# Four chained blocks on one core: norms 1 to 3 in flat steps, low parts one step behind, and the mask and code loads in another order

## What is computed

```
x = x + A0(layernorm(x))     # product with a float32 weight, masked in 32x32 blocks
x = x + F0(layernorm(x))     # product with an int4 weight times a scale, plus a bias
x = x + A1(layernorm(x))     # NF4 weights (16 levels, one scale per 64) with LoRA: q+k+v,
                             # output projection, gate/up with silu, down
x = x + F1(layernorm(x))     # gate/up/down after fake quantisation to fp4 blocks of 16
```

## Time and profile before

| | |
|---|---|
| median of 3 runs | 831.2 us |
| the profiled execution | 829.33 us |
| its span | 828.0 us |
| TensorE (PE) busy | 726.4 us, 88% |
| VectorE (DVE) busy | 569.7 us, 69% |
| ScalarE (ACT) busy | 443.8 us, 54% |
| GpSimd (POOL) busy | 191.2 us, 23% |
| mean TensorE clock granted | 0.955 of full |

### The profile page before, as it was taken

The page is one execution under the profiler, slowest core; times in us unless marked ns, Lnnn a source line. Parts: engine busy times, 40 slices in busy tenths (PEclk is TensorE's granted clock), DMA queues, the critical chain, the costliest instruction groups (busy, mean ns, idle before and its releaser), DMA issues.

```text
span 828.0 us, 11306 instructions
## 1 busy us (share of the span) xinstructions
PE 726.4 (88%) x4136; PEld 538.7 (65%) x4136; DVE 569.7 (69%) x1083; ACT 443.8 (54%) x575; POOL 191.2 (23%) x176
## 2 busy tenths in 40 slices
PE   1898875989999998889998998798999799959998
PEld 1565532656767766657665776575777588947886
DVE  4779976653697788889897985568553434477773
ACT  4778787555876867787666611354322111224542
POOL 0214000021263452535544444122001100000000
PEclk9999966999999999999998999999999899988999
DMA  7736688765466676757655102012001220200001
GB/s 279 223 118 210 198 267 281 249 223 179 133 214 214 203 227 205 238 172 268 216 176 162 65 38 73 26 40 61 16 1 38 61 61 25 65 10 13 25 26 39
DMA packets 56039, 110.55 MB, mean 134 GB/s; under 512 B 9888, under 2 KB 20800, under 8 KB 55984
## 3 DMA queue, kind: packets, MB, share of 16 engines
q1 hardware_dynamic: 42560, 78.43, 29.4%
q10 hardware_dynamic: 9040, 17.30, 6.3%
q0 software_dynamic: 4384, 14.09, 5.9%
HBM read 91.65 MB, written 18.15 MB: 133 GB/s over the span
## 4 chain that ended last, share of the span: by engine, by line
PE 54%; DVE 21%; issue 9%; ACT 8%; DMA 6%; SPq 1%; ACTq 1%; POOL 0%; DVEq 0%; POOLq 0%
PE bank L1122 13%; PE bank L1123 13%; PE bank L1124 13%; PE bank L1229 3%; ACT hot L1528 2%; DVE hot L1774 2%; DVE x L1897 2%; DMA wide_buf<-in_down_flat 2%; DVE bank L1800 2%; PE bank L1417 2%; ACT c L1487 2%; DVE q_a L1847 1%; PE bank L1271 1%; PE bank L1242 1%; DVE q_r L1841 1%
## 5 line engine op out<-in xcount | busy, mean ns | idle before, releaser
L1528 ACT ACTIVATE hot<-rep,levels 128x2048 f16<-128x2048 f16 x96 | 193.6, 2057 | 16.9 <-ACT c L1487 11.0
L1122 PE MATMUL bank<-zt_h,w_h 128*128 128x512 f32 (+1 forms) x232 | 93.3, 402 | 2.5 <-DVE zt_l L1885 2.0
L1124 PE MATMUL bank<-zt_h,w_l 128*128 128x512 f32 (+1 forms) x232 | 91.4, 394 | 0.0
L1123 PE MATMUL bank<-zt_l,w_h 128*128 128x512 f32 (+1 forms) x232 | 91.2, 393 | 0.0
L1229 PE MATMUL bank<-hot,diag 128*32 128x512 f16 x1160 | 79.7, 406 | 2.2 <-ACT hot L1528 2.2
L1122 PE MATMUL bank<-w_h,xq_h 128*128 128x512 f32 (+1 forms) x192 | 74.3, 387 | 5.9 <-DVE w_l L1916 3.6
L1123 PE MATMUL bank<-w_l,xq_h 128*128 128x512 f32 (+1 forms) x192 | 72.0, 375 | 0.0
L1124 PE MATMUL bank<-w_h,xq_l 128*128 128x512 f32 (+1 forms) x192 | 71.9, 375 | 0.0
L2041 POOL TENSOR_TENSOR q_a<-q_a,q_m 128x384 f32<-128x384 f32 (+3 forms) x34 | 35.7, 1051 | 107.6 <-DVE q_m L1668 107.6
L1229 PEld LDWEIGHTS bank<-hot,diag 128*32 128x32 f16 x1160 | 26.4, 100 | 46.3 <-issue 25.7
L2097 POOL TENSOR_TENSOR at_l<-ztok,at_h 128x512 fp32r<-128x512 f32 x28 | 37.4, 1337 | 80.6 <-ACT at_h L1560 80.5
(11 more groups left out here) (222 smaller groups left out, 1688.4 us busy)
## 6 DMA issues: line engine op xcount, KB each, us to landing
rep<-codes SPq DMA_DIRECT2D x58, 512.0 KB, 4.6
codes<-c SPq DMA_DIRECT2D x29, 256.0 KB
raw<-in_codes_gu_t ACTq DMA_DIRECT2D x14, 512.0 KB, 5.7
sc<-in_scales_gu_t SPq DMA_DIRECT2D x56, 128.0 KB, 4.1
raw<-in_codes_attn_t ACTq DMA_DIRECT2D x8, 512.0 KB, 4.4
raw<-in_codes_down_t ACTq DMA_DIRECT2D x7, 512.0 KB, 6.5
sc<-in_scales_down_t SPq DMA_DIRECT2D x28, 128.0 KB, 3.0
wide_buf<-in_gate_flat SPq DMA_DIRECT2D x5, 512.0 KB, 4.2
```

Source lines behind the costliest of these rows:

```text
L1122: PE.matmul(psum, lh, rh, start=first, stop=False, **kw)
L1123: PE.matmul(psum, lh, rl, start=False, stop=False, **kw)
L1124: return PE.matmul(psum, ll, rh, start=False, stop=last, **kw)
L1528: S.activation(hots[plan.slot[hot_ring(t), (t, m)]][:], codes_in_place(t), ACT.Relu, bias=bias, scale=slope).then_inc(sem("ramp_act"), 1)
```

## The change

1. `stages` is written in flat steps: 24 tiles (ln, n) in one sequence and 26 steps. Step s holds the low part of tile s-2, the norm of tile s, the product of tile s-3, the turn of tile s, tsplit of tile s-1, and the add of tile s-4.
2. `PE_LOWS` goes from 3 to 2: norm 3 (ln 2) takes its low parts on VectorE (`tdiff`).
3. The mask: `mask_sum` ahead of `known 0 0`; the weight comes in four loads, and `mask_mul k` waits for its own; the parts of chunks 0 and 1 are made as before by ScalarE and POOL (`MASK_LOWS` = 2), those of chunks 2 and 3 by a copy and a subtraction on VectorE; the first product waits for each chunk where it needs it.
4. Codes and x: `ship 0` is issued on ACT's queue, and x tiles 4 to 7 are loaded on SP's queue behind `spread 0`.
5. Both sides start one step later (`late=1`).
6. `until` leaves its loop before the side step once the weights are there, so the last low parts come ahead of the maximum that stood between.

```diff
-PE_LOWS = 3
+PE_LOWS = 2
+MASK_LOWS = 2
 class Side:
-    def __init__(self, gen, rate=1.0):
-        self.gen, self.rate, self.owed = gen, rate, 0.0
+    def __init__(self, gen, rate=1.0, late=0.0):
+        self.gen, self.rate, self.owed = gen, rate, -late * rate
 ...
         spread(0)
+        p.add("load_rest")
         spread(1)
 ...
             next(nf4)
+            if made[0] > i:
+                break
             for side in sides:
                 side.step()
 ...
+    def turn_step(ln, n):
+        p.add("turn", ln, n)
+        turn_bank(("ln", ln, n), split_done(ln, n))
+    def low_step(ln, n):
+        p.add("tlow" if ln < PE_LOWS else "tdiff", ln, n)
 ...
     def stages():
-        turned = multiplied = added = None
-        for ln, blk in ((0, 1), (1, 2), (2, None)):
-            for n in norm_turn(ln):
-                if ln == n == 0:
-                    for k in range(KD):
-                        p.add("mask_mul", k)
-                if added and added[1] % HN == HN - 1:
-                    known(added[0], added[1] // HN)
-                if turned and turned[0]:
-                    product(*turned)
-                if multiplied and multiplied[0]:
-                    add(*multiplied)
 ...
+        tiles = [(ln, n) for ln in range(3) for n in range(NT)]
+        def behind(step, by):
+            return tiles[step - by] if 0 <= step - by < len(tiles) else None
+        for step in range(len(tiles) + 2):
+            now, high, low, ready, multiplied = (behind(step, by) for by in range(5))
+            if low:
+                low_step(*low)
+            if now:
+                norm(*now)
+            if step == 0:
+                for k in range(KD):
+                    p.add("mask_mul", k)
+                for k in range(KD):
+                    p.add("mask_low" if k < MASK_LOWS else "mask_rest", k)
+            if ready and ready[0] < 2:
+                product(ready[0] + 1, ready[1])
+            if now:
+                turn_step(*now)
+            if high:
+                p.add("tsplit", *high)
+            if multiplied and multiplied[0] < 2:
+                add(multiplied[0] + 1, multiplied[1])
+            if step < HN // 2:
+                stats(0, HN + 2 * step)
+                stats(0, HN + 2 * step + 1)
+            yield
 ...
+    p.add("mask_sum")
     known(0, 0)
-    p.add("mask_sum")
-    weave(stages(), Side(itertools.chain(int4_weights(), greatest), INT4_RATE), Side(ready_nf4, EARLY_RATE))
+    weave(stages(), Side(itertools.chain(int4_weights(), greatest), INT4_RATE, 1), Side(ready_nf4, EARLY_RATE, 1))
 ...
+                    if blk_no == 1:
+                        pe.wait_ge(*masked(k))
 ...
+            elif kind == "mask_rest":
+                dve.wait_ge(*done("dve", "mask_mul", k))
+                steady.up(V.tensor_copy(wring[0][0][:, k, :], wraw[:, k, :]))
+                steady.wait_ge()
+                V.tensor_tensor(wring[0][1][:, k, :], wraw[:, k, :], wring[0][0][:, k, :], ALU.subtract).then_inc(
+                    sem("mask_rest_dve"), 1)
 ...
+            elif kind == "ship" and key[0] == 0:
+                act.wait_ge(*done("act", "cast", 0))
+                S.dma_start(rooms[0].rearrange("u p n -> p u n"), c16[:]).then_inc(dma_sem(("codes", 0)), 16)
 ...
-                SP.dma_start(wraw, a["weight_t"].rearrange("(k p) n -> p k n", p=P)).then_inc(dma_sem("weight"), 16)
+                weight_v = a["weight_t"].rearrange("(k p) n -> p k n", p=P)
+                for k in range(KD):
+                    SP.dma_start(wraw[:, k, :], weight_v[:, k, :]).then_inc(dma_sem(("weight", k)), 16)
 ...
+            elif kind == "load_rest":
+                for n in range(HN, NT):
+                    SP.dma_start(x[:, n, :], x_d[:, n, :]).then_inc(dma_sem(("x", n)), 16)
```

More of the change, by code:

```diff
@@ L511, in norm_turn @@
         for n in range(NT):
-            p.add("turn", ln, n)
-            turn_bank(("ln", ln, n), split_done(ln, n))
-            if ln < PE_LOWS and turned is not None:
-                p.add("tsplit", ln, turned)
+            turn_step(ln, n)
             if n + 1 < NT:
                 norm(ln, n + 1)
-            if ln >= PE_LOWS and turned is not None:
+            if turned is not None:
                 p.add("tsplit", ln, turned)
-            if turned is not None:
-                p.add("tlow" if ln < PE_LOWS else "tdiff", ln, turned)
+                low_step(ln, turned)
                 yield turned
@@ L1049, in weight_vacant, with masked @@
         return None
+    def masked(k):
+        return done("pool", "mask_low", k) if k < MASK_LOWS else done("dve", "mask_rest", k)
     def x_settled(ln, n):
@@ L1686, in dve_program @@
                 dve.wait_ge(*done("dve", "mask_keep"))
-                dve.wait_ge(*landed("weight"))
+                dve.wait_ge(*landed(("weight", k)))
                 wk = wraw[:, k, :].rearrange("p (b c) -> p b c", c=32)
```

29 lines of the change are left out of this document (11 added, 18 removed).

## The result

The changed kernel takes 836.57 us (median of 7 runs, 833.67 to 839.09) beside 831.2 us (7 runs, 828.14 to 833.9) for the kernel before on the same chip: ratio 1.0063, 95% interval 1.0039 to 1.0087. It is slower by 0.6%; 823.7 was forecast. The profiled execution took 836.57 us, its span 835.1 (before 828.0).

What follows compares the result with a forecast made beforehand. TensorE was taken to bound 31 to 63 us, VectorE 55 to 91, a ring with ScalarE behind 91 to 142.5. Terms -1.5, 0, -0.5, -5, -1.5, +1 gave -7.5: 831.2 to 823.7 us, range 815 to 832.

Steps and rivals of the forecast that it cites:

- term 6: Attention: two maxima (one, if nine are left) moved into it, mostly covered by TensorE's steps; +1 us, bounds 0 and +8.9.
- terms 3 to 5: From 55 us to the attention's start: VectorE's stretch to 91 us -0.5, then -5 to 142.5, last low parts -1.5.
- term 1: The front: earlier masking brings block 1's first product to 23.1 from 25.40, partly lost between products; -1.5 us, bounds 0 and -4.4.
- rival C: VectorE's queue between `merge` and `assemble`: ten maxima in the attention, each at its load's pace, cost 8.9; 833.6 us, chance 0.13.
- term 4: 91 to 142.5 us: ScalarE loses eight low parts and its `tlow` waits, VectorE takes the subtractions; -5 us, two slower looks +2.1.
- the first sign that I had named: Block 1's first product on TensorE (L1122) would start at about 23 us instead of 25.4.
- the ring: 91 to 142.5 us: TensorE, ScalarE and VectorE wait for each other around `tsplit` and `tlow`; breaking it was part of -5.
- rival A: Ahead of the attention: VectorE becomes the bound through eight added subtractions; -3.0 us, 828.2, chance 0.18 shared with an unbroken ring.
- term 5: End of the attention weights: last low part ahead of the maximum, at 140.35 instead of 141.84; -1.5 us, bounds -1.0 and -2.5.
- Term 2: 31 to 63 us: TensorE bounds block 1's products and its work stays the same; 0 us, bounds 0 and -0.6.

Runs made afterwards that it cites:

- e9: Changed kernel, ten maxima still in the attention, but the 17th moved behind its step's look-up work instead of ahead of the first four `o_take`: 830.17 us, 0.9977.
- e13: Changed kernel with the NF4 side starting two steps late instead of one and INT4_RATE 0.66 instead of 0.6, seven maxima left in the attention: 822.81 us, 0.9898.
- e1: Changed kernel with INT4_RATE 0.72 instead of 0.6, so seven maxima are left in the attention instead of ten: 828.88 us, 0.9936.
- e11: Changed kernel with INT4_RATE 0.72 and x tiles 4 to 7 loaded behind the LoRA loads instead of ahead: ratio 0.9940.
- e5: Changed kernel without the break in `until`, so nine maxima are left in the attention: ratio 0.9985 to the kernel before.
- e6: Kernel before with the break alone (low parts ahead of the last maximum), nine maxima left in the attention: ratio 0.9992.
- e8: Changed kernel with INT4_RATE 0.72 and `PE_LOWS` 3, so norm 3's low parts are again by TensorE and ScalarE: ratio 0.9969.
- e10: Changed kernel with INT4_RATE 0.72 and the NF4 side starting two steps late instead of one, six maxima left in the attention: 820.83 us, 0.9865.
- e12: Kernel before with INT4_RATE 0.65 instead of 0.6, so seven maxima are left in the attention: 830.06 us, 0.9976.
- e16: Kernel before with INT4_RATE 0.66 and the NF4 side one step late, seven maxima left in the attention: ratio 1.0055.
- e4: Kernel before with the flat steps and both sides one step later, without the new front, `PE_LOWS` 3, no break: ratio 1.0056.
- e3: Kernel before with `PE_LOWS` 2 alone, norm 3's low parts by VectorE in the old steps: ratio 1.0004.

## Why the prediction was wrong

The profile moved by +7.1 where -7.5 was forecast. Of these 14.6 us, term 6 has 6.0, terms 3 to 5 have 4.9, term 1 has 2.3, and 1.4 lie in the part that nothing edits.

**Term 6 failed, and by the most.** It priced the maxima moved into the attention at +1; the way grew by 7.0. (+8.9 was only the bound that rival C would need.) The step that failed is the price by number, "a maximum's reduction is 1.2 and TensorE's steps of 2.9 cover it", as it takes no account of what stands behind each one. The ways of all kernels grow slowly with the number left: 49.1 and 49.5 with four, 52.1 to 55.1 with seven, 55.4 to 57.6 with nine, some 1.4 us each. The tenth adds 5.5 to 7.8 to the ways with nine, and with it moved e9 is at 56.3. It put a maximum that waits 4.22 us for its load ahead of `o_take` and `assemble`. That is C's place (VectorE's queue ahead of `assemble`), but not C's price list. I had divided 35.5 us by 8, the time of a stretch by the maxima in it, instead of writing down which instruction stands behind the last one.

Two limits of this account. Against the kernel before, the waits for `assemble` did not grow: 4.1 us in three, one of them 3.03 behind a maximum that waited 6.11, against 3.9 in one. What grew is TensorE's busy time, by 3.4, the wait at the way's end, by 2.4, and the one for `at_l`, by 1.3 (1.4 to 2.7). And for those 2.4 us, ScalarE's start at 202.48, the cause stays open.

**The slower matmuls were in no term.** Of the 7.0 us, TensorE's idle time is 11.0 - 7.5 = 3.5 and its busy time 52.17 - 48.73 = 3.4 for the same work, with the granted clock at 0.87 instead of 0.93. Behind the idle 3.86 at 187.99 the matmuls took 0.63 instead of 0.39, and the granted clock of that stretch is 0.50, the lower level (1.2 GHz):

```profile
188.50:191.00 2.50, 2.50 (x7) 1.96 (x6) 2.47 (x6) 1.70 (x3) 0.49 (x2) 0.50 0.45 139
```

The Trainium skill ("TensorE: Matmul & The Clock Gate", section "HAM oscillation — how this bites in real kernels") states that matmul bursts parted by long waits run at the half clock; I had applied it to the look-ups of term 4, where it did not decide, and the trace agrees with it here. It does not follow every wait in this study, though: see the last section.

**Term 1 (-1.5) came out as +0.8.** The first product was better than forecast (22.08 against 23.1), and the first sign that I had named came true, while the second product came 2.9 later than before. The step "TensorE has to wait between its first products, where I put 0.8" is the one that failed: the first NF4 step held ScalarE for 3.22 + 1.03 of waits and a ramp of 2.09. I had priced its instructions and not the loads it waits for. e13 against e1 measures that at 3.8 us, and e11 shows that sooner LoRA loads are no remedy, since x is behind them on the same queue. (The sum for the first product also took the norms at 0.6 each, the time of a copy; they take 0.81.)
The first copy beside POOL's subtraction took 1.49 us, the second 0.42, an extra 1.1 as I had allowed on that place.
The Trainium skill ("SBUF — State Buffer", section "Who interferes with whom") lets fast VectorE copies and POOL exclude each other; the trace agrees with those two rows.

**Terms 3, 4 and 5 (-0.5, -5, -1.5) came out together as -2.1.** What they described happened: ScalarE's wait for the low matmul fell from 4.9 to 1.5, VectorE took the subtractions, and no maximum stands at the end. The bound was wrong: VectorE was busy 44.34 and not the 42.3 of my sum (in 55 to 91 us it had done 1.4 less than before), with 50.20 available, so it had only 5.9 of idle left, and 2.2 + 1.8 of these were waits for ScalarE's high parts (L1764, L1845). New waits took the ring's place: ScalarE stood 8.0 us for `mv` instead of 1.3, since on a fuller VectorE the reciprocal came late, and TensorE 3.4 + 3.3 for the LoRA matmul instead of 2.2 + 0.3. The prediction had the root chain as "bare" and priced it in the stretch before, not here. What the wait for `mv` cost is not shown: it is 7.9 in e1 and 2.9 in e13, and both take 75.7 from block 2 to `merge_mm`. In the main that is rival A, which I held at 0.18; my argument against it, 11.6 us of idle, did not ask whether that idle lay where the new work arrives. e5 and the changed kernel put term 5 at 1.9, e6 and the kernel before at nothing. e8 against e1 puts `PE_LOWS` in the flat steps at 3.6, where term 4 had 5.

**Term 2** held: TensorE was busy 31.76 of 32.00 from 31 us on, if part of it at the lower clock (0.95 granted instead of 1.00).

## What to carry to other kernels

When side work is moved from one stage to another, count where its last item lands in the in-order queue, and write down what stands directly behind it: the cost here rose by some 1.4 us an item, and by 5.5 to 7.8 us at the one item that landed in the wrong place (2.4 of that unexplained). A faster first instruction proves nothing; look at the second and third, and at every load that the instructions between them wait for. Once an order has changed, the rates and delays tuned for the old order must be set again: the same change is +0.6% with the old numbers and -1.35% with two new ones (e10), while in the old order a higher rate alone brought 0.24% (e12), and with a later start it made the kernel slower (e16).

## What was not expected of the hardware

The wait of 3.9 us on TensorE cost more than itself: the LoRA matmul behind it and the seven next took about 1.6 us longer than in e9, where that wait is 0.7. But no price per us of wait follows. At the same kind of place, in front of a LoRA matmul of the attention, the matmuls were slow behind waits of 2.69 us in e4, 2.70 in e5 and 3.03 in the kernel before, and not slow behind 2.60 in e6 and 2.83 in e3. So a wait on the engine that bounds can bring a slow stretch with it, and the price is a range from nothing to that. And the last big maximum's load was issued at 177.32 and reduced at 182.79: 5.5 us for 512 KB, with the last load sent right behind it.
